# Splitting the mixed rows of routing weights into eight transfers and issuing the first weights from two queues

## The chip, the core and the metric

The kernel runs on one core of one Trainium2 chip. The metric is the device time of one execution in microseconds (us), and the time before is the median of three runs. Engines are called as the profile calls them: PE (TensorE matmul), PEld (its weight load), DVE (VectorE), ACT (ScalarE), POOL (GpSimd) and SP (SyncE, which issues the DMA transfers).

## What is computed

The reference takes x of 32 x 256 tokens of 128 numbers and adds two blocks to it, each behind a layer normalisation. Cut to what matters:

```python
# block 1: a selective state space layer, d_inner = 256, 16 states per channel
u, res = split(norm(x) @ W_in); u = silu(u)
delta = softplus(u @ W_delta + b_delta); Bm = u @ W_B; Cm = u @ W_C
h = exp(delta * A) * h + delta * Bm * u      # for every token in turn
y = (sum over states of h * Cm + u * D) * silu(res)
x = x + y @ W_out
# block 2: a mixture of 8 experts of 341 hidden units, 4 chosen per token, and one shared expert
weights = softmax of the 4 largest of norm(x) @ Wg + bias, 0 for the others
out = shared(norm(x)) + sum over experts of weights[e] * W3[e] (silu(W1[e] x) * (W2[e] x))
```

## The kernel before

The 8192 tokens are worked through in 16 tiles of 512. Every engine runs one long list of steps (`SP_ORDER`, `PE_ORDER`, `ACT_ORDER`, `DVE_ORDER`, `POOL_ORDER`); an entry such as `1:bbc.5` is step `bbc`, number 5, of tile 1. The lists interleave block 2 of one tile with block 1 of the next. Engines meet by semaphores alone, and an engine that waits holds up everything behind it in its list.

The nine experts (the shared one first) have 9 x 341 = 3069 hidden units, padded to 24 groups of 128 rows. They are laid in three groups of three experts; in each group six row groups belong to one expert whole, and the last two hold the 85 remaining units of each of the three experts, one after the other. A step `gated` on DVE multiplies two projections for a row group, `wmul` on POOL (L904) multiplies two row groups at once by the routing weight of their expert for each token, and `w3` on PE (L1331) projects them into `eo_bank`. Where both row groups are of one expert, SP spreads one row of 512 weights over 128 partitions (`wb`, L794, 256 KB). Where they are mixed (three steps per tile, 48 in all), `wb_mixed` of 2 x 128 partitions is filled from three rows, by four transfers whose partition counts stand in `SPANS` (L41): 85, 43, 42 and 85 (L804). There is one buffer `wb_mixed`, and the next fill waits until POOL has used it. The same `SPANS` cut the loads of W3 (L736).

Block 1 goes through `bbc` (L768): SP spreads two rows of Bm over 128 partitions (512 KB), POOL multiplies them into `hb` (`dbu`, L875), DVE runs the recurrence on `hb` (`scan`, L1077), and PE turns the result (`turn`, L1265). The buffers of `bbc` form a ring of four.

At the start SP issues x of tile 0, the small weights, then W1 and W2 (`load_w1_w2`, six transfers each, 1.5 MB each) and only then x of tile 1. DVE takes the statistics of tile 1 (`ln`, L1036), copies `c_sb` (L1070) and then splits W1 and W2 into a high and a low part (`split`, L1047 and L1049). POOL makes the scale of the normalisation of tile 1 from the statistics (`rstd`, L840 to L848) ahead of `delta` (L861), `du` (L866) and the first `dbu` of tile 0.

## Time and profile before

| | us |
|---|---|
| median of three runs | 1477.82 (1477.6 to 1478.57) |
| profiled execution | 1480.54 |
| its span on the core | 1478.7 |

| engine | busy in the span, us | share |
|---|---|---|
| PE | 1390.2 | 94% |
| DVE | 1297.3 | 88% |
| ACT | 1219.0 | 82% |
| POOL | 1193.2 | 81% |

The span is what the profile sees from the first instruction to the last; the profiled execution is 1.84 us longer. Busy shares are means over a start, a middle in which two tiles overlap, and an end; what the change may do is to be read from the places in which an engine stands idle and from what ended the wait. SP has no busy time of its own here: issuing a transfer or waiting isn't counted as work.

### The profile page before, as it was taken

The numbers are of one execution on the slowest core, as the hardware profiler recorded it, in microseconds if no ns is written. First come the engines' busy times: TensorE is split into PE (matmuls) and PEld (weight loads), VectorE is DVE, ScalarE is ACT, GpSimd is POOL, SyncE is SP. The second block draws the span as 40 slices with busy tenths as digits, with TensorE's granted clock in tenths as the row PEclk, the third lists the DMA queues.
The fourth block names the chain that finished last, engine by engine and source line by source line (L and its number), as shares of the span: only waits on it lengthen the run. The fifth ranks groups of instructions, "written<-read, shape, count | busy, mean of one in ns | idle before, by whom it ended". The sixth has DMA issues, their size and how long they took to land.

```text
span 1478.7 us, 28297 instructions
## 1 busy us (share of the span) xinstructions
PE 1390.2 (94%) x8950; PEld 1167.4 (79%) x8950; DVE 1297.3 (88%) x2444; ACT 1219.0 (82%) x1753; POOL 1193.2 (81%) x655
## 2 busy tenths in 40 slices
PE   5976699999999999999999999999899999999999
PEld 3854588888878888887878788787788878788888
DVE  3839899899989999999999999999899999989642
ACT  5977598888987989998888998999788889899431
POOL 5937697988969798988979889896898979697454
PEclk8987899999999999999999999999999999999999
DMA  6503141416144161514244051432314142232221
GB/s 176 159 8 107 66 127 58 145 45 170 46 123 129 43 174 44 172 37 143 88 111 126 32 186 51 138 100 86 121 59 146 37 151 94 83 119 77 67 67 49
DMA packets 88219, 146.40 MB, mean 99 GB/s; under 512 B 11306, under 2 KB 42791, under 8 KB 88071
## 3 DMA queue, kind: packets, MB, share of 16 engines
q1 hardware_dynamic: 88070, 144.59, 32.1%
q8 instruction: 73, 1.20, 0.3%
q14 instruction: 76, 0.61, 0.1%
HBM read 139.55 MB, written 5.01 MB: 98 GB/s over the span
## 4 chain that ended last, share of the span: by engine, by line
PE 59%; POOL 9%; DMA 9%; issue 9%; DVE 6%; ACT 5%; SPq 3%; DVEq 0%; POOLq 0%; ACTq 0%
PE eo_bank L1331 16%; PE turn L1265 9%; PE shared L1317 8%; PE shared L1319 8%; PE shared L1318 8%; POOL hb L875 4%; DMA bbc<-b_rows 4%; POOL gated L904 3%; DVE hb L1077 3%; PE shared L1222 3%; DMA wb_mixed<-w_rows 2%; DMA wb<-w_rows 2%; DVE acc L1089 2%; PE shared L1230 1%; PE shared L1293 1%
## 5 line engine op out<-in xcount | busy, mean ns | idle before, releaser
L1077 DVE TENSOR_TENSOR_SCAN hb<-decay,hb 128x512 f32<-128x512 f32 x512 | 607.4, 1213 | 43.8 <-POOL hb L875 36.2
L875 POOL TENSOR_TENSOR hb<-soft,bbc 128x1024 f32<-128x1024 f32 x256 | 605.9, 2383 | 48.0 <-issue 22.1
L1331 PEld LDWEIGHTS eo_bank<-w_sb,gated 128*128 128x128 f32 x3072 | 400.9, 193 | 65.1 <-POOL gated L904 24.7
L1331 PE MATMUL eo_bank<-w_sb,gated 128*128 128x128 f32 x3072 | 424.5, 277 | 18.8 <-POOL gated L904 18.6
L1011 ACT ACTIVATE decay<-delta,a_sb 128x510 f32<-128x510 f32 x512 | 342.6, 687 | 91.2 <-DVE hb L1077 88.5
L928 ACT ACT_TABLE_LOAD x315 | 404.1, 1283 | 5.6
L1089 DVE SCALAR_TENSOR_TENSOR acc<-turn,c_sb,acc 128x256 f32<-128x256 f32 x900 | 381.8, 476 | 16.0 <-PE turn L1265 15.2
L904 POOL TENSOR_TENSOR gated<-gated,wb 128x1024 f32<-128x1024 f32 x128 | 304.3, 2383 | 74.5 <-DVE gated L1159 48.9
L1265 PE MATMUL turn<-ident,hb 128*128 128x128 f32 x2048 | 304.9, 277 | 25.9 <-DVE acc L1089 16.4
L1265 PEld LDWEIGHTS turn<-ident,hb 128*128 128x128 f32 x2048 | 245.3, 143 | 79.1 <-issue 40.3
L1159 DVE TENSOR_TENSOR gated<-shared,s 128x512 f32<-128x512 f32 x384 | 257.3, 682 | 57.2 <-PE shared L1319 41.5
L1021 ACT ACTIVATE s<-shared 128x512 f32<-128x512 f32 x384 | 218.2, 597 | 103.8 <-PE shared L1319 80.3
L1317 PE MATMUL shared<-xh,w1h 128*128 128x512 f32 x384 | 176.2, 459 | 5.5 <-DVE gated L1159 5.0
L1317 PE MATMUL shared<-xh,w2h 128*128 128x512 f32 x384 | 177.3, 462 | 4.2 <-DVE gated L1159 3.6
L1319 PE MATMUL shared<-xh,w1l 128*128 128x512 f32 x384 | 152.9, 398 | 0.0
L1319 PE MATMUL shared<-xh,w2l 128*128 128x512 f32 x384 | 152.6, 397 | 0.0
L1318 PE MATMUL shared<-xl,w1h 128*128 128x512 f32 x384 | 152.4, 397 | 0.0
L1318 PE MATMUL shared<-xl,w2h 128*128 128x512 f32 x384 | 152.2, 396 | 0.0
L904 POOL TENSOR_TENSOR gated<-gated,wb_mixed 128x1024 f32<-128x1024 f32 x48 | 114.3, 2381 | 24.4 <-DMA wb_mixed<-w_rows 16.2
L1317 PEld LDWEIGHTS shared<-xh,w1h 128*128 128x128 f32 x384 | 73.4, 191 | 22.1 <-DVE gated L1159 8.6
L1319 PEld LDWEIGHTS shared<-xh,w1l 128*128 128x128 f32 x384 | 72.8, 190 | 17.6
L1319 PEld LDWEIGHTS shared<-xh,w2l 128*128 128x128 f32 x384 | 72.7, 189 | 17.5
(96 smaller groups left out, 1323.6 us busy)
## 6 DMA issues: line engine op xcount, KB each, us to landing
bbc<-b_rows SPq DMA_DIRECT2D x128, 512.0 KB, 5.8
wb<-w_rows SPq DMA_DIRECT2D x128, 256.0 KB, 6.6
wb_mixed<-w_rows SPq DMA_DIRECT2D x96, 170.0 KB
wb_mixed<-w_rows SPq DMA_DIRECT2D x48, 86.0 KB
x_in<-x_dram SPq DMA_DIRECT2D x16, 256.0 KB, 2.9
x_cur<-x_dram SPq DMA_DIRECT2D x16, 256.0 KB, 5.6
wb_mixed<-w_rows SPq DMA_DIRECT2D x48, 84.0 KB
out_dram<-o SPq DMA_DIRECT2D x15, 256.0 KB, 5.8
```

Of the source, the lines that this page charges most:

```text
L875: pool.tensor_tensor(hb[:, arg % HB_RING, :, :], du[:, h, :].unsqueeze(1).broadcast_to((P, GN, TOK)), bbc[:, r, :].rearrange("p (n t) -> p ...
L904: pool.tensor_tensor(tiles, tiles, weight, ALU.mult).then_inc(weighed, 1)
L928: act.preload_act_table_set(table)
L1011: act.activation(decay_bank[i][:, :].rearrange("p (b t) -> p b t", t=SEQ)[:, :, 1:], delta[:, h, :].rearrange("p (b t) -> p b t", t=SEQ)[: ...
L1077: dve.tensor_tensor_scan(states, decay_bank[i][:, :], states, 0.0, ALU.mult, ALU.add)\
L1089: dve.scalar_tensor_tensor(acc[:, blk, :], turn_bank[pair][:, i * DI:(i + 1) * DI], c_sb[:, blk, n:n + 1], acc[:, blk, :], ALU.mult, ALU.add)\
L1159: dve.tensor_tensor(gated[:, arg % GATED_RING, :], bank_of(t, "h2", arg)[:, :], s[:, arg % S_RING, :], ALU.mult).then_inc(gated_ready, 1)
L1265: mm = pe.transpose(turn_bank[pair][:, (NH * i + h) * P:(NH * i + h + 1) * P], src[:, blk * P:(blk + 1) * P], ident[:, :])
L1317: pe.matmul(dst[:, :], hi[:, cols], xh[:, :], start=True, stop=False)
L1318: pe.matmul(dst[:, :], hi[:, cols], xl[:, :], start=False, stop=False)
L1319: pe.matmul(dst[:, :], lo[:, cols], xh[:, :], start=False, stop=True).then_inc(full[step], 1)
L1331: mm = pe.matmul(eo_bank[:, blk * P:(blk + 1) * P], gated[:, k % GATED_RING, blk * P:(blk + 1) * P], w3_sb[:, k, :], start=(arg == 0 and k ...
```

## The change

`SPANS` gets eight entries instead of four: the pieces of 85, 43, 42 and 85 partitions become 80 + 5, 32 + 11, 32 + 10 and 80 + 5, with their place in the expert's remaining rows written out. Each piece has a semaphore of its own, so POOL waits for eight before a mixed `wmul`, and `w_out` on SP tests eight instead of four. The loads of W3 are cut the same way. The six transfers of W1 go from SP's list to ACT's, right behind its first table load; W2 stays on SP. Six waits on ACT name an earlier signal than before (the PE step that fills a bank in place of the engine that read it). The lists of steps are unchanged.

```diff
@@ -38,7 +38,8 @@
 WEIGHED = PAIRS - 1
 WHOLES = [q - 1 for q in range(1, PAIRS) if q % GROUP_PAIRS < GROUP]
 MIXED = [q - 1 for q in range(1, PAIRS) if q % GROUP_PAIRS == GROUP]
-SPANS = [(0, 0, REST, 0), (0, REST, P, 1), (1, 0, 2 * REST - P, 1), (1, 2 * REST - P, 3 * REST - P, 2)]
+SPANS = [(0, 0, 80, 0, 0), (0, 80, 85, 0, 80), (0, 85, 117, 1, 0), (0, 117, 128, 1, 32),
+         (1, 0, 32, 1, 43), (1, 32, 42, 1, 75), (1, 42, 122, 2, 0), (1, 122, 127, 2, 80)]
 
 HB_RING = 8
 BB_RING = 4
@@ -690,6 +691,18 @@
         SMALL = 8
         CONSTS = 8
         SUMS = 2 * FILLS - 4
+
+        def load_halves(eng, dst, src, landed, cleared):
+
+            eng.wait_ge(blank, cleared)
+            by_group = dst.rearrange("p (g c) -> p g c", g=GROUPS)
+            src_of = src.rearrange("p (g i c) -> p g i c", g=GROUPS, i=GROUP)
+            for grp in range(GROUPS):
+                eng.dma_start(by_group[:, grp, 0:GROUP * WHOLE].rearrange("p (i c) -> p i c", i=GROUP),
+                              src_of[:, grp, :, 0:WHOLE]).then_inc(landed, 16)
+                eng.dma_start(by_group[:, grp, GROUP * WHOLE:GROUP * HID].rearrange("p (i c) -> p i c", i=GROUP),
+                              src_of[:, grp, :, WHOLE:]).then_inc(landed, 16)
+
         block = ctx.enter_context(nc.Block())
 
 
@@ -709,18 +722,6 @@
                     sp_eng.dma_start(dst, src).then_inc(small_in, 16)
                 assert len(small) == SMALL
 
-            def load_w1_w2():
-
-                sp_eng.wait_ge(blank, 2)
-                for dst, src, landed in ((stage, w1_all, w1_in), (stage2, w2_all, w2_in)):
-                    by_group = dst.rearrange("p (g c) -> p g c", g=GROUPS)
-                    src_of = src.rearrange("p (g i c) -> p g i c", g=GROUPS, i=GROUP)
-                    for grp in range(GROUPS):
-                        sp_eng.dma_start(by_group[:, grp, 0:GROUP * WHOLE].rearrange("p (i c) -> p i c", i=GROUP),
-                                         src_of[:, grp, :, 0:WHOLE]).then_inc(landed, 16)
-                        sp_eng.dma_start(by_group[:, grp, GROUP * WHOLE:GROUP * HID].rearrange("p (i c) -> p i c", i=GROUP),
-                                         src_of[:, grp, :, WHOLE:]).then_inc(landed, 16)
-
             def load_w3():
 
                 sp_eng.wait_ge(blank, 3)
@@ -729,10 +730,8 @@
                     for j in range(WHOLE // P):
                         sp_eng.dma_start(w3_by_group[:, g_, j:2 * GROUP:2, :], w3_of[j * P:(j + 1) * P, g_, :, :])\
                             .then_inc(w3_in, 16)
-                taken = [0] * GROUP
-                for tile, lo, hi, i in SPANS:
-                    at = WHOLE + taken[i]
-                    taken[i] += hi - lo
+                for tile, lo, hi, i, at in SPANS:
+                    at += WHOLE
                     sp_eng.dma_start(w3_by_group[lo:hi, :, 2 * GROUP + tile, :], w3_of[at:at + hi - lo, :, i, :])\
                         .then_inc(w3_in, 16)
 
@@ -744,7 +743,7 @@
                         sp_eng.dma_start(x_in[:, :, :], x_t[:, TT * t:TT * (t + 1), :]).then_inc(x_in_sem, 16)
                         if t == 0:
                             load_small()
-                            load_w1_w2()
+                            load_halves(sp_eng, stage2, w2_all, w2_in, 2)
                     elif step == "load_cur":
                         wait_if(sp_eng, x1_ready, t)
                         carry_waits(sp_eng)
@@ -800,7 +799,7 @@
                                 sp_eng.wait_ge(consts, CONSTS)
                             wait_if(sp_eng, weighed, WEIGHED * (t + old // len(MIXED)) + MIXED[old % len(MIXED)] + 1)
                             carry_waits(sp_eng)
-                            for part, (tile, lo, hi, i) in enumerate(SPANS):
+                            for part, (tile, lo, hi, i, _) in enumerate(SPANS):
                                 sp_eng.dma_start(wb_mixed[lo:hi, tile, :],
                                                  rows[GROUP * grp + i, :].partition_broadcast(hi - lo))\
                                     .then_inc(wb_mixed_in[part], 16)
@@ -927,16 +926,16 @@
                         table = TABLE_OF[step]
                         act.preload_act_table_set(table)
                     if step == "xn":
-                        wait_if(act, xnT_ready, t)
+                        wait_if(act, full["xT"], t)
                         normalize("x", x_in, xn, t)
                     elif step == "x1n":
-                        wait_if(act, xl_ready, t)
+                        wait_if(act, full["x1T"], t)
                         normalize("x1", x1[:, t % 2, :, :], x1n, t)
                     elif step == "xT":
-                        wait_if(act, sres_ready, NH * t)
+                        wait_if(act, full["wi_res"], NH * t)
                         read_bank(t, step, arg, xnT[:, :], ACT.Copy, xnT_ready)
                     elif step == "x1T":
-                        wait_if(act, gate_steps, GATE_STEPS * t)
+                        wait_if(act, full["gate"], t)
                         read_bank(t, step, arg, x1nT[:, :], ACT.Copy, x1T_ready)
                     elif step == "xh":
 
@@ -948,8 +947,8 @@
                     elif step == "wi":
                         wait_if(act, du_ready, t)
                         wait_if(act, ud_ready, NH * t)
-                        wait_if(act, cbT_ready, t)
-                        wait_if(act, zb_ready, NH * t)
+                        wait_if(act, full["bt"], t)
+                        wait_if(act, full["dz"], NH * t)
                         read_bank(t, step, arg, u[:, arg, :], ACT.Silu, wi_ready)
                     elif step == "ud":
                         act.wait_ge(wi_ready, NH * t + arg + 1)
@@ -980,7 +979,7 @@
                         read_bank(t, step, arg, sres[:, arg, :], ACT.Silu, sres_ready)
                     elif step == "bt":
                         wait_if(act, b_stored, 16 * TT * t)
-                        wait_if(act, c_ready, t)
+                        wait_if(act, full["ct"], t)
                         act.wait_ge(full["bt"], t + 1)
                         act.activation(cbT[:, :], bank_of(t, "bt", 0)[:, 0:P], ACT.Copy).then_inc(cbT_ready, 1)
                     elif step == "wT":
@@ -1021,6 +1020,7 @@
                         act.activation(s[:, arg % S_RING, :], bank_of(t, "h1", arg)[:, :], ACT.Silu).then_inc(s_ready, 1)
 
             act.preload_act_table_set(EXP_TABLE)
+            load_halves(act, stage, w1_all, w1_in, 1)
             act.wait_ge(a_in, 16)
             act.activation(a_sb[:, :, :], a_sb[:, :, :], ACT.Exp).then_inc(a_exped, 1)
             act.wait_ge(consts, CONSTS)
```

SP's list in the middle of the program, at a mixed step of tile 1 (`wb` and `wb_mixed` carry routing weights, `bbc` carries Bm), before:

```order
L768 DMA bbc<-b_rows 128x1024 x2
L804 DMA wb_mixed<-w_rows 85x512
L804 DMA wb_mixed<-w_rows 43x512
L804 DMA wb_mixed<-w_rows 42x512
L804 DMA wb_mixed<-w_rows 85x512
L794 DMA wb<-w_rows 128x512 x2
L768 DMA bbc<-b_rows 128x1024
```

and now:

```order
L767 DMA bbc<-b_rows 128x1024 x2
L803 DMA wb_mixed<-w_rows 80x512
L803 DMA wb_mixed<-w_rows 5x512
L803 DMA wb_mixed<-w_rows 32x512
L803 DMA wb_mixed<-w_rows 11x512
L803 DMA wb_mixed<-w_rows 32x512
L803 DMA wb_mixed<-w_rows 10x512
L803 DMA wb_mixed<-w_rows 80x512
L803 DMA wb_mixed<-w_rows 5x512
L793 DMA wb<-w_rows 128x512 x2
L767 DMA bbc<-b_rows 128x1024
```

Eight issues stand where four stood, ahead of the same transfers. The start of ACT's list now (`gated` is the memory in which W1 waits to be split):

```order
L1022 ACT_TABLE_LOAD
L701 DMA gated<-w_all_dram 128x3x256
L703 DMA gated<-w_all_dram 128x3x85
L701 DMA gated<-w_all_dram 128x3x256
L703 DMA gated<-w_all_dram 128x3x85
L701 DMA gated<-w_all_dram 128x3x256
L703 DMA gated<-w_all_dram 128x3x85
L1025 ACTIVATE a_sb<-a_sb 128x32
```

Before, these six stood on SP between the small weights and W2, and ACT had nothing between its table load and `a_sb`.

## Rows read from the trace of the kernel before

**Rows 1.** Busy time by stretch, the middle: us, then each engine, PEclk, DMA share, GB/s.
```profile
240.00:1365.00 1125.00, 1097.12 (x7113) 920.31 (x7111) 1068.41 (x2029) 995.17 (x1392) 964.86 (x515) 1.00 0.33 102
```

**Rows 2.** Waits of POOL: who, for what, us in total, times, longest.
```profile
POOL gated L904 <- DMA wb<-w_rows: 24.6, 8, 6.1
POOL hb L875 <- issue: 22.1, 6, 5.2
...
POOL gated L904 <- DMA wb_mixed<-w_rows: 16.2, 7, 5.0
```

**Rows 3.** Line L804: issue ns min/median/max; then L768, bbc: issue to landing.
```profile
L804 SPq DMA_DIRECT2D wb_mixed<-w_rows x192: 258/297/1426, 134.9 to 1454.9; - x192
...
DMA to landing us min/median/max: 3.3/5.8/14.2
```

**Rows 4.** Chain of waits at 1362 us: start, us, what.
```profile
1362.02 10.52 DMA wb_mixed<-w_rows
```

**Rows 5.** Busy time by stretch around that transfer, columns as in group 1.
```profile
1361.00:1364.00 3.00, 3.00 (x19) 2.47 (x18) 3.00 (x5) 2.87 (x5) 0.98 (x1) 1.00 0.93 281
...
1370.00:1373.00 3.00, 2.99 (x21) 2.52 (x19) 3.00 (x6) 1.40 (x3) 0.30 (x1) 1.00 0.08 30
```

**Rows 6.** Timeline of POOL at two waits: start, us, what, [idle before, what ended it].
```profile
149.50 2.34 POOL L875 TENSOR_TENSOR hb<-soft,bbc 128x1024 f32<-128x1024 f32 x1 [4.71 <-issue]
...
269.05 2.35 POOL L904 TENSOR_TENSOR gated<-gated,wb_mixed 128x1024 f32<-128x1024 f32 x1 [2.57 <-DMA wb_mixed<-w_rows]
```

**Rows 7.** Timeline of PE at the six places of the middle and the end.
```profile
271.45 1.16 PE L1331 MATMUL eo_bank<-w_sb,gated 128*128 128x128 f32 x8 [2.35 <-POOL gated L904]
...
444.64 0.50 PE L1317 MATMUL shared<-xh,w2h 128*128 128x512 f32 x1 [3.01 <-DVE gated L1159]
...
782.83 0.71 PE L1331 MATMUL eo_bank<-w_sb,gated 128*128 128x128 f32 x4 [1.58 <-POOL gated L904]
...
1242.34 0.63 PE L1265 MATMUL turn<-ident,hb 128*128 128x128 f32 x4 [1.39 <-DVE acc L1089]
...
1299.79 1.16 PE L1331 MATMUL eo_bank<-w_sb,gated 128*128 128x128 f32 x8 [1.71 <-POOL gated L904]
...
1375.10 2.04 PE L1331 MATMUL eo_bank<-w_sb,gated 128*128 128x128 f32 x8 [2.11 <-POOL gated L904]
```

**Rows 8.** Busy time by stretch behind two of these places.
```profile
270.00:276.00 6.00, 4.55 (x17) 3.73 (x18) 2.75 (x5) 3.18 (x4) 6.00 (x3) 0.72 0.30 104
...
1375.00:1378.00 3.00, 2.90 (x11) 2.71 (x12) 0.00 (x0) 0.00 (x0) 3.00 (x3) 0.53 0.40 66
```

**Rows 9.** Chain of waits at the start: x of tile 1, from its issue to its landing.
```profile
13.71 5.89 DMA x_in<-x_dram
```

**Rows 10.** Busy time by stretch at the start, columns as in group 1.
```profile
6.00:9.00 3.00, 2.66 (x22) 2.47 (x21) 0.00 (x0) 1.65 (x4) 0.64 (x2) 1.00 0.64 132
...
12.00:15.00 3.00, 3.00 (x8) 1.33 (x7) 0.00 (x0) 2.31 (x4) 0.00 (x0) 1.00 1.14 315
```

**Rows 11.** Timeline of the start: PE, then DVE, then POOL.
```profile
18.74 0.30 PE L1247 MATMUL shared<-ident,cbT 128*128 128x128 f32 x1 [0.49 <-ACT cbT L985]
...
20.70 0.19 DVE L1070 COPY c_sb<-shared 128x64 f32<-128x64 f32 x1
...
22.59 3.36 DVE L1049 TENSOR_TENSOR w1l<-gated,w1h 128x3072 fp32r<-128x3072 f32 x1
...
27.65 3.36 DVE L1049 TENSOR_TENSOR w2l<-hb,w2h 128x3072 fp32r<-128x3072 f32 x1
38.31 2.34 DVE L1077 TENSOR_TENSOR_SCAN hb<-decay,hb 128x512 f32<-128x512 f32 x2 [7.30 <-POOL hb L875]
...
22.68 3.32 POOL L842 TENSOR_SCALAR negm_x<-mv_x 128x4 f32<-128x4 f32 x1
...
31.03 2.34 POOL L861 TENSOR_TENSOR delta<-delta,soft 128x1024 f32<-128x1024 f32 x1
```

**Rows 12.** DMA issues by line: KB each, median us from issue to landing.
```profile
b_rows<-cbT SPq DMA_DIRECT2D x64, 8.0 KB, 1.4
```

## The prediction

> **What bounds the kernel now.** I read the busy time by stretch first. In the middle, from 240 to 1365 us, PE is busy for 1097 of 1125 us and DVE for 1068 [rows 1]: two engines near their limit, with 28 us of idle time on PE. A gain there must come from places where both stand still, so the next view is who makes them wait. POOL is the engine between them, and its waits [rows 2] name transfers three times: 24.6 us for `wb`, 16.2 us for `wb_mixed`, and 22.1 us before `hb` that the profile calls "issue". These last I count as waits for `bbc`: a `dbu` needs only `bbc`, `du` and free `hb` buffers, and nothing on an engine ended then.
>
> The transfers explain the length of these waits. The chain at 1362 us runs through the last of four `wb_mixed` transfers, which takes 10.52 us from issue to landing [rows 4]. Its three mates were issued right before it, and all four bring 255 rows of 2 KB, 510 KB. A `bbc` of 512 KB lands in 3.3 us when nothing lies ahead of it, and in up to 14.2 us [rows 3]. Size is not the reason. The reader is to compare the DMA share in the first and the last 3 us of the transfer: 0.93 of the 16 DMA engines at first, 0.08 at the end [rows 5]. 0.08 of 16 is little more than one engine: the fill ends with one DMA engine working through its part while the others have nothing left. Rows of 85 and 43 partitions are evidently not dealt out evenly to 16 engines, and whatever is issued behind them lands late too.
>
> **Mixed rows, the main term.** 80 and 32 partitions divide by 16, and the pieces left over are 5, 11, 10 and 5. If the 510 KB are dealt out evenly, the fill lands no sooner than a lone `bbc` (3.3 us) and no later than now (10.5 us). Four more issues at the median of 0.30 us [rows 3] come on top, 1.2 us. I take a landing about 5 us earlier: 7.2 us of possible gain less 1.2, less 1 because the DMA engines are nearly full of other traffic at the beginning [rows 5]. Transfers queued right behind gain some 4 us.
>
> What that is worth I read where POOL stood waiting with a mixed fill in flight, and what PE lost behind it:
> - At 149.5 us POOL waits 4.71 us for the `bbc` issued right behind the first mixed fill, then runs one more `wmul` for which PE waits [rows 6]: 4.7 us.
> - At 269 us POOL waits 2.57 us for the fill itself [rows 6], and PE idles 2.35 us. At five more places PE idles 3.01, 1.58, 1.39, 1.71 and 2.11 us behind the same pattern [rows 7]; sometimes DVE stands between POOL and PE, as at 444.6 and 1242.3 us. The six gaps are 12.15 us.
> - Behind the first and the last of them PE's granted clock is lower, 0.72 over 6 us and 0.53 over 3 us [rows 8], which is the lower of its two levels (1.2 and 2.4 GHz) for part of the time; PE had stood idle just before in both. (1 - 0.72) x 6 + (1 - 0.53) x 3 = 3.1 us, if PE had worked through all of it.
>
> That is 4.7 + 12.15 + 3.1 = 20.0 us if every one of these vanishes and nothing takes its place. The other end is zero. I take two thirds, 13.3 us: DVE and PE idle together at most of these places, so the loss is real, but PE has only 28 us of idle time in the whole middle and DVE 57 [rows 1], and the lists keep an order in which the next wait is often for another engine. Work that piled up in a pause will in part wait elsewhere.
>
> The price is on SP. 48 mixed fills with four more issues make 48 x 1.2 = 58 us of SP's time, hidden behind the waits in which SP stands anyway; where it isn't hidden, the next `bbc` or `wb` is issued 1.2 us later and still lands earlier than now. Four more tests ahead of `w_rows` in each tile, and four more semaphores ahead of 48 `wmul` (the queue of POOL tests them while the multiplication before still runs), I put at 1 us in all, between 0 and 3.
>
> **W1 on ACT's queue, and the start.** x of tile 1 is issued at 13.71 us, behind W1 and W2, and lands 5.89 us later, at 19.6 us [rows 9]. From 12 to 15 us the DMA engines are full at 315 GB/s, from 6 to 9 us they move 132 GB/s [rows 10]. With W1 issued from ACT right behind its first table load, the empty part is filled: at least 3 us x (315 - 132) GB/s = 0.55 MB, which is 1.7 us less to do later, and about twice that if the 3 us before are as empty. I take 3 us: x of tile 1 lands at about 16.6 us. For the six issues on ACT I put nothing: its own first work waits for x and the scale of tile 0, and idles longer than six issues take. The small weights share the DMA engines with W1 now; tile 0 needs them only some us later.
>
> What follows is less than 3 us. DVE then waits for `ct` from PE, which ends at 18.74 + 0.30 = 19.04 us, instead of x, and copies `c_sb` at 19.2 instead of 20.70 us [rows 11]: the split is 1.5 us earlier. POOL makes the scale of tile 1 before the split begins and not beside it. Beside it, an operation on four numbers per partition took 3.32 us, from 22.68 to 26.00 us, and ended with DVE's subtraction, which took 3.36 us from 22.59 us [rows 11]. So POOL stands still while DVE splits. The page "SBUF — State Buffer" of the Trainium skill (section "SBUF: two separate sides") states it as a lock on a shared port, held for a whole instruction, against a DVE instruction with two inputs in SBUF; by that rule `delta` and `du` can't run beside the split either, and the start gains about 1.5 us and no more. The trace agrees as far as the small operations show it.
>
> `delta` starts at 31.03 us, when the split ends at 27.65 + 3.36 = 31.01 us, and the first recurrence at 38.31 us after an idle time of 7.30 us on DVE [rows 11]. The low end is thus 1.5 us (POOL still waits for the split's end); the high end 1.5 + 7.3 = 8.8 us (`delta`, `du` and `dbu` fit beside the split). I take 2.5 us, near the low end, since the row shows POOL stopped; the extra 1 us is for ACT, which no longer has tile 1's normalisation between the split and its first decays. The moved waits on ACT cost and save nothing: none of the signals that they replace ended a wait of ACT that counts.
>
> **The sum.** 13.3 + 2.5 - 1 = 14.8 us off the profiled execution of 1480.5 us, 1465.7 us. The median of the runs lies 2.7 us below that execution, so the prediction is **1463 us**.
>
> **Rivals.**
> - *Mostly hidden.* Only the waits that the profile ascribes to `wb_mixed` vanish. On PE these are the gaps at 271, 783 and 1375 us, 2.35 + 1.58 + 2.11 = 6.0 us [rows 7]; two thirds are 4 us: 1474 us. For it speaks that 16.2 of POOL's waits bear that name and 24.6 us the name of `wb` [rows 2], many of these right behind `w_rows` with no fill ahead. Against it, that the `bbc` behind a fill lands late as well [rows 3, 6]. Chance 0.16, of which 0.06 ends within 3 us of no change; that the pieces aren't dealt out evenly after all, so that nothing happens, is in it with 0.02.
> - *More than that.* All 20 us come off, and POOL works beside the split: 20 + 8.8 = 28.8 us off 1477.8 us, 1449 us. Against it stands the row of POOL stopped beside the split, and that lists kept as they are rarely give back every gap. Chance 0.12.
> - *Slower: eight issues delay what stands behind them.* POOL's 8 + 6 + 7 waits for transfers [rows 2] each become 1.2 us longer, 25 us on POOL; a third of it reaching PE is 8 us: 1486 us. It decides if the landing of a fill gains less than the 1.2 us that its issue loses. The page "DMA: Bandwidth & Descriptors" of the Trainium skill (section "Rules for kernel authors") says to join many small transfers into a large one, since under 64 KB one pays mostly overhead; six of the eight pieces are 64 KB or less, so by this rule the case would be likely. Against it stands that transfers of 8 KB land in 1.4 us [rows 12], less than half the time of a `bbc` alone, and are issued one right behind the other: their overheads overlap. Chance 0.06.
>
> The forecast keeps 0.66.
>
> **The numbers.** A measurement of this kernel tells about 0.2% (3 us) from no change. Faster by more: 0.66 + 0.12 + 0.10 = 0.88; within: 0.06; slower: 0.06. The range runs from 1451 us, most of the way to the larger case, to 1474 us, where only the named waits go; outside lie most of the slower case, the smallest effects and the far end of the larger one, together less than 0.2.
>
> **What would show it.** Right: POOL's waits for `wb_mixed` near zero and those for `wb` and "issue" at most half; the longest landing of a `bbc` well under 14.2 us; PE's gaps at the six places gone or under 1 us, its clock whole there; x of tile 1 landed near 16.6 us, POOL's scale of tile 1 done before the split, the first recurrence at about 36 us. Wrong: POOL's waits for transfers vanish and the span hardly moves (then POOL wasn't what held PE, and waits for DVE or for PE's own list will have grown by the same amount); or the fills still take 10 us; or the longest waits now stand behind SP's eight issues.

## The result, and the profile after

The changed kernel takes **1445.99 us** (median of four runs, 1444.51 to 1446.87) against 1478.19 us for the kernel before, run beside it (1477.6 to 1483.46): a ratio of 0.9773, 95% interval [0.975, 0.9797]. I had forecast 1463 us with a range of 1451 to 1474. The sign is right and the size is not: 32 us came off where I expected 15, and the time lies below the range. The profiled execution took 1446.87 us, its span 1445.1 us, 33.6 us less than before.

The page's first part, then the shares of the chain that ended last (by engine):

```profile
PE 1381.1 (96%) x8950; PEld 1164.5 (81%) x8950; DVE 1296.5 (90%) x2444; ACT 1218.0 (84%) x1753; POOL 1194.7 (83%) x655
...
PE 74%; DVE 9%; issue 6%; ACT 4%; POOL 3%; DMA 2%; SPq 1%; DVEq 0%; ACTq 0%; POOLq 0%
```

PE's busy time fell by only 9 us (1390.2 before), its idle time by some 25 us (1478.7 - 1390.2 = 88.5 before, 64.0 now). On the chain, PE's share rose from 59% to 74%, while DMA fell from 9% to 2% and POOL from 9% to 3%. The middle of the span, to compare with [rows 1] (us, then busy us of PE, PEld, DVE, ACT and POOL, then PEclk, DMA share, GB/s):

```profile
240.00:1330.00 1090.00, 1077.86 (x7042) 908.19 (x7042) 1056.26 (x2008) 983.89 (x1379) 958.14 (x509) 1.00 0.33 104
```

PE stands idle for 12 of 1090 us here, against 28 of 1125. Who waits on POOL, to compare with [rows 2] (us in total, times, longest):

```profile
POOL gated L903 <- DMA wb<-w_rows: 24.4, 8, 5.5
...
POOL hb L874 <- DMA bbc<-b_rows: 14.4, 5, 7.0
...
POOL hb L874 <- PE turn L1265: 6.9, 3, 3.8
POOL hb L874 <- issue: 5.5, 3, 2.8
```

No wait for `wb_mixed` is left (16.2 us before), and "issue" fell from 22.1 to 5.5 us. The waits for `wb` are as long as before, 24.4 us, while I had named a fall to half as a sign of being right: they don't follow the fills. Now the transfers: the eight pieces (line L803, issue ns and landing us, min/median/max), then `bbc` (L767), to compare with [rows 3]:

```profile
L803 SPq DMA_DIRECT2D wb_mixed<-w_rows x384: 269/321/1124, 133.6 to 1422.9; - x192
...
DMA to landing us min/median/max: 1.8/2.8/6.6
...
DMA to landing us min/median/max: 3.3/4.8/8.6
```

A piece lands within 6.6 us, where the one of [rows 4] took 10.52, and the longest `bbc` takes 8.6 instead of 14.2 us. The DMA engines during the first mixed fill of tile 14, the last but one (issued from 1331.40, landed at 1337.62; columns as above), show why. It is the same fill as in [rows 5]:

```profile
1331.00:1334.00 3.00, 3.00 (x19) 2.51 (x18) 3.00 (x5) 2.73 (x4) 0.63 (x1) 1.00 0.85 269
1334.00:1337.00 3.00, 3.00 (x21) 2.43 (x20) 3.00 (x6) 2.97 (x5) 3.00 (x2) 1.00 0.77 245
1337.00:1340.00 3.00, 3.00 (x23) 2.74 (x23) 3.00 (x6) 2.97 (x4) 1.22 (x2) 1.00 0.55 184
```

The share is 0.85 and 0.77 while the fill is in flight, where it had run down from 0.93 to 0.08; the third row already holds what comes behind it. The long tail at a share of little more than one engine is gone.

Next the places of [rows 6] and [rows 7]. Of the six gaps of PE, five are gone altogether and one has 0.36 us left (430.80, the one of 3.01 us at 444.64). At the two places of POOL no idle time is recorded any more. This is POOL's timeline, then the PE gap that is left behind the first place (2.26 us, where it was 6.99 at 154.20 us before, so the 4.7 us forecast there came off):

```profile
143.38 2.36 POOL L874 TENSOR_TENSOR hb<-soft,bbc 128x1024 f32<-128x1024 f32 x1
...
260.32 2.40 POOL L903 TENSOR_TENSOR gated<-gated,wb_mixed 128x1024 f32<-128x1024 f32 x1
...
148.10 0.99 PE L1331 MATMUL eo_bank<-w_sb,gated 128*128 128x128 f32 x4 [2.26 <-POOL gated L903]
```

PE's granted clock, which had been at its lower level for 3.4 us from 166.9, 3.4 us behind the gap at 271 us, 6.8 us from 1040.7 and 3.4 us from 1375, is at the lower level for one stretch of 3.4 us at 1022 in the whole of 166 to 1445 us.

The start went otherwise than forecast (the chain's row of x of tile 1; busy time from 6 to 9 us; then DVE and POOL, to compare with [rows 9 to 11]):

```profile
11.99 6.59 DMA x_in<-x_dram
```

```profile
6.00:9.00 3.00, 3.00 (x18) 3.00 (x17) 0.18 (x1) 1.77 (x5) 0.74 (x2) 1.00 1.18 311
```

```profile
19.68 0.19 DVE L1070 COPY c_sb<-shared 128x64 f32<-128x64 f32 x1
...
26.64 3.36 DVE L1049 TENSOR_TENSOR w2l<-hb,w2h 128x3072 fp32r<-128x3072 f32 x1
37.30 2.34 DVE L1077 TENSOR_TENSOR_SCAN hb<-decay,hb 128x512 f32<-128x512 f32 x2 [7.31 <-POOL hb L874]
...
19.95 1.64 POOL L839 TENSOR_SCALAR veps_x<-mv_x 128x4 f32<-128x4 f32 x1 [13.13 <-DVE mv_x L1040]
21.67 3.32 POOL L841 TENSOR_SCALAR negm_x<-mv_x 128x4 f32<-128x4 f32 x1
...
30.01 2.34 POOL L860 TENSOR_TENSOR delta<-delta,soft 128x1024 f32<-128x1024 f32 x1
```

The DMA engines are full from 6 us on (311 GB/s, before 132), as meant. But x landed at 18.6, not 16.6 us, and the first recurrence starts at 37.30 instead of 38.31 us: 1.0 us gained, not 2.5. POOL still makes its scale beside the splits (`negm_x` again takes 3.32 us). A cost that I had put at nothing shows here, too: `a_sb`, which now shares the DMA engines with W1, lands at 7.03 instead of 4.56 us, and ACT starts tile 0's normalisation behind it at 7.19 instead of 6.84 us (6.88 in e1 below, where W1 stays on SP).

I matched every instruction of PE in the two traces and read how far it moved (the lists have the same length and order). The table sums that by stretch of the span before, in us, for the changed kernel and for six of the runs below, which the next section explains.

```
stretch before    changed   e2     e3     e6     e5     e4     e9
   0 to   45       -1.2    -0.9   -1.5   -1.3   -1.6   -0.9   -0.2
  45 to  130       -0.1     0.0   +1.8   -0.2   +0.1   -0.8   +1.5
 130 to  200       -4.8     0.0   -1.0   -1.7   -3.5   -4.8   -4.5
 200 to  300       -4.1    -2.0   -1.8   -2.7   -4.1   -4.0   +1.3
 300 to  600       -4.4    -2.0   -4.1   -5.4   -5.2   -4.3   +1.5
 600 to  800       -2.7    +1.8   -1.1   -2.9   -3.1   -3.1   +3.8
 800 to 1070       -5.2    -0.1   -2.1   -6.0   -7.4   -1.9   -4.8
1070 to 1475      -11.2    -0.2   -2.2   -9.6  -10.6   -6.6   +1.1
sum               -33.7    -3.3  -12.0  -29.7  -35.3  -26.4   -0.2
```

One row of the changed kernel stood nowhere in my prediction: 5.2 us between 800 and 1070, nearly all of it between 1034 and 1066. Single entries of a microsecond or two are to be read with care: e2 has the old pieces and the old time, and still moves by up to 2.0 us in a stretch.

### The profile page after: what moved, and what is told of

Its sections match the earlier page's. It is cut to its first block, busy times and chain, and to the rows that moved or that the text cites. A ratio compares the mean times of both kernels' runs of the same rounds, so it can differ in the third digit from the quotient of the medians.

```text
span 1445.1 us, 28645 instructions
## 1 busy us (share of the span) xinstructions
PE 1381.1 (96%) x8950; PEld 1164.5 (81%) x8950; DVE 1296.5 (90%) x2444; ACT 1218.0 (84%) x1753; POOL 1194.7 (83%) x655
## 4 chain that ended last, share of the span: by engine, by line
PE 74%; DVE 9%; issue 6%; ACT 4%; POOL 3%; DMA 2%; SPq 1%; DVEq 0%; ACTq 0%; POOLq 0%
PE eo_bank L1331 20%; PE turn L1265 12%; PE shared L1317 10%; PE shared L1319 10%; PE shared L1318 10%; DVE hb L1077 5%; PE shared L1222 3%; DVE acc L1089 2%; PE shared L1230 2%; PE shared L1293 2%; POOL hb L874 1%; ACT L927 1%; POOL gated L903 1%; PE eo_bank L1276 1%; PE shared L1276 1%
## 5 line engine op out<-in xcount | busy, mean ns | idle before, releaser
L874 POOL TENSOR_TENSOR hb<-soft,bbc 128x1024 f32<-128x1024 f32 x256 | 606.9, 2389 | 27.9 <-DMA bbc<-b_rows 14.4
L903 POOL TENSOR_TENSOR gated<-gated,wb_mixed 128x1024 f32<-128x1024 f32 x48 | 114.7, 2389 | 10.3 <-DVE gated L1159 10.2
L1319 PEld LDWEIGHTS shared<-xh,w2l 128*128 128x128 f32 x384 | 72.2, 188 | 17.3
```

The lines of the kernel that those rows point to most:

```text
L874: pool.tensor_tensor(hb[:, arg % HB_RING, :, :], du[:, h, :].unsqueeze(1).broadcast_to((P, GN, TOK)), bbc[:, r, :].rearrange("p (n t) -> p ...
L903: pool.tensor_tensor(tiles, tiles, weight, ALU.mult).then_inc(weighed, 1)
L1319: pe.matmul(dst[:, :], lo[:, cols], xh[:, :], start=False, stop=True).then_inc(full[step], 1)
```

## The experiments

Each run was timed beside the kernel before, whose median was 1479.87 us for e1 to e4, 1480.59 for e5 to e8, 1480.22 for e9 to e11 and 1480.92 for e12, against 1478.19 above. So between these groups, and against the changed kernel, the ratios compare better than the times.

**One part alone.** e1 is the kernel before with the eight even pieces and nothing else. e2 is the changed kernel with the four old pieces:

```diff
 # e2, against the changed kernel
-SPANS = [(0, 0, 80, 0, 0), (0, 80, 85, 0, 80), (0, 85, 117, 1, 0), (0, 117, 128, 1, 32),
-         (1, 0, 32, 1, 43), (1, 32, 42, 1, 75), (1, 42, 122, 2, 0), (1, 122, 127, 2, 80)]
+SPANS = [(0, 0, 85, 0, 0), (0, 85, 128, 1, 0), (1, 0, 42, 1, 43), (1, 42, 127, 2, 0)]
```

> The kernel before with nothing changed but the eight even pieces (routing weights and W3); W1 stays on SP, ACT's waits as before. Theory (the even pieces free the last DMA engine, W1 on ACT gives only the 1.2 us that the start moved): 1447 us, ratio 0.979. Rival (W1 from ACT, or the earlier signals that ACT waits for, bring the part of the gain that the prediction missed, about 15 us): 1462 us, ratio 0.99.

> The changed kernel with the four old pieces of 85, 43, 42 and 85 put back; W1 on ACT and ACT's new waits stay. Theory: 1.0 to 1.3 us below before, about 1477 us, ratio 0.999, with POOL's waits as before. Rival (as in the first run): about 1463 us.

e1 took 1447.02 us, ratio 0.9778 [0.9764, 0.9791]; e2 1478.65 us, ratio 0.9991 [0.9981, 1.0001] (its profiled execution lies 3 us lower than the one before, its median doesn't). The pieces are the change; W1 on the second queue and ACT's new waits are worth about 1 us, and by the interval 3 at most. In e1 DVE's first recurrence starts at 38.33 us as before, in e2 at 37.38 us as in the changed kernel, so the 1.0 us of the start is W1's.

**Even, or just more?** The length of a fill, here and below, is the time from the first issue to the last landing of its pieces, the median over the 48 fills. Rows per DMA engine follow from how many engines each transfer shows at its landing: 85 rows go to 5 engines, 43 to one, 42 to 14, 80 and 32 to 16. Which engines these are the traces don't name, but one, called engine 0 here, must be in all: in each of the 48 fills before, the pieces land one after the other, the 43 rows 3.9 us behind the first 85, the 42 (3 on an engine) 0.24 us behind these and the last 85 (17 on an engine) another 1.4 us later (medians), some 0.08 to 0.09 us per row. This engine gets 17 + 43 + 3 + 17 = 80 of 255 rows before, 18 in the changed kernel. (The others are counted as if a transfer always took the first ones.) The page "DMA: Bandwidth & Descriptors" of the Trainium skill (section "Why a DMA increments its semaphore by 16 and not by 1") gives the rule: the largest number up to 16 that divides the slowest dimension (of more than one element) on both sides. The trace agrees in each of these sizes. e3 has eight pieces, too, cut so that engine 0 still gets 80 rows (75 + 10 + 37 + 6 + 29 + 13 + 75 + 10). e4 leaves the second and third fill of each tile in four old pieces and cuts only the first evenly.

> The changed kernel with eight pieces per mixed fill that are cut badly on purpose: 75, 10, 37, 6, 29, 13, 75, 10 partitions. 37 and 29 have no divisor up to 16, so if a transfer uses the largest number of engines up to 16 that divides its partitions, one engine gets 5 + 1 + 37 + 1 + 29 + 1 + 5 + 1 = 80 of the 255 rows, as many as with the four old pieces (17 + 43 + 3 + 17), and 18 with the changed kernel's pieces. Theory (what counts is the fullest engine): 1476 to 1481 us, like before less the start, fills that end 10 to 12 us after their issue. Rival (smaller or more pieces bring the gain): 1446 us.

> The changed kernel in which only the first of a tile's three mixed fills is cut into eight even pieces; the second and the third use the four old pieces. Theory (the gain comes from a few places, nearly all behind a tile's first fill, whose use follows its issue by 11 to 17 us, where the second and third have 15 to 25 us): 5 to 7 us slower than the changed kernel, 1451 to 1453 us; what comes back is mainly at tile 12's second fill (1.6 us) and behind tile 10's second (2.4 us). Rival (a shorter time in the queue helps everywhere alike): a third of the gain, 1467 us.

e4 came close to what was expected, 0.7 us above the range: 1453.72 us, 0.9823 [0.981, 0.9836]. The first fill of a tile carries most of the gain; in most tiles of the kernel before it is issued 11 to 17 us ahead of its multiplication, the second and third mostly 14 to 25 us. e3 fell between theory and rival: 1468.35 us, 0.9921 [0.9908, 0.9935]. Its fills last 10.0 us (10.6 before), and `bbc` lands within 11.9 us of its issue (14.2 before). So number alone does little to a fill, and yet a third of the gain came with fills that are 0.6 us shorter: PE's gaps of over 0.3 us behind 165 us sum to 24.7 us against 30.8, and the time at the lower clock behind 200 us fell from 13.6 to 6.8 us. Besides the 80 rows on engine 0, e3 takes load off engines 1 to 4 (37 rows before, at most 14 in e3). Whether that, the order of the pieces or the 1.5 us more that SP takes to issue them brought this third stays open, so the fullest engine is shown for the length of a fill and not for all of the time.

**How even is enough?** e5 and e6 have six pieces each, with 40 rows on each of five engines, and 58 rows on one.

```diff
 # pieces of a fill, rows
-80 + 5 + 32 + 11 + 32 + 10 + 80 + 5
+85 + 32 + 11 + 32 + 10 + 85            # e5: engines 0 to 4 get 40
+80 + 5 + 43 + 42 + 80 + 5              # e6: engine 0 gets 58
```

> The mixed fill in six pieces, 85 + 32 + 11 + 32 + 10 + 85 rows: the two pieces of 85 still go to five engines (17 rows each), the middle is even, so engines 0 to 4 get 40 rows each of a fill and the rest get 4 to 6. Theory (the time follows the rows on the fullest engine: 80 gave 1468 to 1479, 18 gave 1447): a fill lasts about 7 us and the time is about 1454 (1450 to 1459), better than 58 rows on one engine. Rival (what matters is that some engines carry the load at all, or that the load is taken off engines 1 to 4): 1462 or more, no better than the kernel with 58 rows on engine 0 alone.

> The mixed fill in six pieces, 80 + 5 + 43 + 42 + 80 + 5 rows: the big pieces are even, the middle one of 43 rows goes to engine 0 alone, so engine 0 gets 58 rows and no other more than 14. Theory (rows on the fullest engine): a fill lasts about 8.5 us, the time is about 1461 (1456 to 1466), some 7 us over the kernel with 40 rows on five engines. Rival (the five-engine pieces were the harm, the single-engine piece is not): 1450 or less, under the kernel with 40.

e5 took 1445.72 us, 0.9761 [0.9745, 0.9777], the whole gain; e6 1450.74 us, 0.9796 [0.9779, 0.9813]. The order of the two is the theory's; both are far faster than I expected, as I had drawn a straight line through the times. Fills get shorter with every step, the times do not. (A fill is counted as landing at its use if its last piece lands within 0.5 us ahead of POOL's multiplication.)

```
rows on the fullest engine       80   80 (e3)   58 (e6)   40 (e5)  18 (changed)
median fill, us                10.6      10.0       7.8       6.4           5.2
first fill of a tile, us       11.8      11.6      10.1       7.9           6.1
fills landing at their use        8         8         5         2             0
PE gaps over 0.3 us            30.8      24.7       9.4       6.2           8.3
time, us                     1478.2    1468.4    1450.7    1445.7        1446.0
ratio to before              1.0000    0.9921    0.9796    0.9761        0.9773
```

A row on the fullest engine lengthens a fill by (10.0 - 7.8) / 22 = 0.10 us from 58 to 80 rows, and by 0.08 and 0.05 us in the steps below. From 10.6 to 7.8 us of fill, each us is worth 10 us of time; below 6.4 us nothing is left to gain. That is the shape of a due time: the fill, with what is issued behind it, has to be there when POOL comes. The traces bear it out: POOL stands idle for 16.5 us at the eight fills that land at their use before, and for 0.02 us at the two that still do in e5.

**Is a transfer behind the fill what is late?** e9 is the kernel before, uneven pieces and all, with `bbc` issued ahead of a fill at the 18 places where it had come within 3 us behind one. One of them:

```diff
-10:wbc.0.1 12:b_out.0 10:wbc.2.3 12:bbc.0 10:wbc.4 12:bbc.1
+10:wbc.0.1 12:b_out.0 12:bbc.0.1 10:wbc.2.3.4
```

> The kernel before with its four uneven pieces, and one thing moved: at the 18 places where an input broadcast bbc is issued on SP within 3 us behind a mixed fill, it is issued ahead of the fill. The fills stay as long (10.6 us); what stood behind them no longer does. Theory (part of the 33 us came from bbc transfers that had waited behind a fill's long pieces on the same DMA engines, which my prediction didn't count, above all near 1034 to 1066): 8 to 15 us faster than before, 1465 to 1472, with the 5 us near 1034 to 1066 gone and POOL's waits for wb_mixed still near 16 us. Rival (the fills' own lateness is all that counts): no change, 1477 to 1481, or slower, as the fills then start later.

The time stayed, 1480.24 us, ratio 1.0001 [0.9988, 1.0014], so my 8 to 15 us fell. The table of stretches shows two effects that cancel. From 130 to 200 us e9 gains 4.5, and from 800 to 1070 us 4.8, as much as the changed kernel does there. From 200 to 800 and behind 1070 us it loses 7.7 us, where the fills are issued later and POOL waits longer for them. (Ahead of 130 us nothing was moved; the 1.5 us there are the spread between traces.) POOL's waits in e9:

```profile
POOL gated L903 <- DMA wb_mixed<-w_rows: 29.7, 10, 5.9
...
POOL hb L874 <- issue: 9.2, 3, 4.9
```

"issue" fell from 22.1 to 9.2 us, and `wb_mixed` rose from 16.2 to 29.7. So both readings hold, each at its own places: at those two it is the `bbc` behind the fill that is late, elsewhere the fill itself. Moving all 18 doesn't serve both, and a shorter fill does; moving `bbc` at those two places alone wasn't tried. e9 also tells what the profile's name hid. This is POOL before, near 1034 and 1055 us:

```profile
1034.30 4.68 POOL L875 TENSOR_TENSOR hb<-soft,bbc 128x1024 f32<-128x1024 f32 x2 [4.04 <-PE turn L1265]
...
1055.06 2.40 POOL L875 TENSOR_TENSOR hb<-soft,bbc 128x1024 f32<-128x1024 f32 x1 [4.43 <-issue]
```

and the PE gap that follows the first of them, and the stretch behind it, in which PE runs at 1.2 GHz (PEclk 0.50):

```profile
1039.76 0.50 PE L1317 MATMUL shared<-xh,w1h 128*128 128x512 f32 x1 [3.64 <-DVE gated L1159]
```

```profile
1040.70:1047.50 6.80, 6.16 (x23) 5.45 (x23) 5.22 (x9) 3.76 (x5) 6.80 (x4) 0.50 0.51 145
```

The `bbc` needed at 1034.30 was issued at 1023.64, 0.9 us behind a fill, and its last part landed at 1034.18, after 10.5 us. In the changed kernel the same one takes 5.9 us. The profile put the wait down to a PE step, I passed over it, and PE's 3.64 us and half of 6.8 us at the lower clock went uncounted. (In the changed kernel 0.83 us of this gap and 3.4 us at the lower clock are left.)

**The price of an issue.** e10 has the fill in twelve even pieces, 18 rows on the fullest engine as in eight, and four more issues (48 + 32 + 5, 16 + 16 + 11, 16 + 16 + 10, 48 + 32 + 5).

> The changed kernel with the mixed rows in twelve even pieces (48+32+5, 16+16+11, 16+16+10, 48+32+5 rows): the rows per engine stay as in eight, the issues of SP grow by four per fill, some 1.5 us. Six pieces with at most 40 rows on one engine already gave the whole gain. Theory (SP's issues and the number of transfers are hidden): 1445 to 1448. Rival (the count of transfers is a price of its own, which fewer rows per engine only outweighs): 1451 or more.

The result is the rival's: 1452.74 us, 0.981 [0.9785, 0.9835], 7 us over eight pieces by the medians and 5.5 by the ratios. (The two intervals overlap by 0.001; the slowest run of the changed kernel and of e1 took 1448.94 us, the fastest of e10 1451.46.) A fill takes 4.8 us to issue (3.0 in eight pieces, 1.3 in four), and SP reaches the next transfer later. The fills themselves last 6.3 us, as long as in e5, where that cost nothing. At the same place the `dbu` behind a first fill waits longer (POOL in the changed kernel, then in e10):

```profile
426.44 2.40 POOL L874 TENSOR_TENSOR hb<-soft,bbc 128x1024 f32<-128x1024 f32 x1 [2.51 <-issue]
```

```profile
429.75 2.39 POOL L873 TENSOR_TENSOR hb<-soft,bbc 128x1024 f32<-128x1024 f32 x1 [3.98 <-issue]
```

In both the `bbc` lands just before (426.32 and 429.63 us). PE loses 1.4 us behind this place, of the 8.8 us between the two traces; the largest part, 3.1 us, lies between 650 and 700 us. This is the mechanism of my slower rival, with too little weight to show at eight. The Trainium skill's page "DMA: Bandwidth & Descriptors" (section "Rules for kernel authors") advises joining small transfers; the runs agree from eight to twelve and disagree from four to eight, where evenness was worth some 30 us more than the issues cost.

**The start.** e7 issues x of tile 1 ahead of W2. e8 does that as well and moves the split of W1 on DVE from before the first recurrence to behind tile 0's last; the waits that count the splits change with it.

```diff
 # e7, SP, tile 0 and tile 1
                             load_small()
+                        elif t == 1:
                             load_halves(sp_eng, stage2, w2_all, w2_in, 2)
 # e8 besides, DVE
-0:c.0 0:split.0.1 0:scan0.0
+0:c.0 0:split.1 0:scan0.0
...
-3:ln.0 0:x1.0
+3:ln.0 0:split.0 0:x1.0
```

> The changed kernel with tile 1's x issued ahead of W2. Its x should land near 13 instead of 18.6, so that the small operations of its normalization are done before DVE's splits begin. If x's landing is what the first recurrence hangs on (my prediction's reasoning), the first recurrence starts some 5 us sooner, near 32 in the span, and the time falls by 3 to 5 us to about 1442. Rival: the splits themselves keep POOL's operations from running beside them, whenever x lands; the first recurrence then stays at 36 to 37.5 and the time at 1445 to 1446.5.

> As the kernel with tile 1's x first, but one of the two 6.7 us splits moves on DVE from before the first recurrence to before tile 0's gate input (W2's is then the first, W1's the later). If DVE's splits are what delays the first recurrence, it starts near 31 instead of 37.3 and the time falls by 4 to 6 us against the changed kernel, to about 1441. Rival: the split costs DVE the same 6.7 us wherever it stands, since DVE and TensorE's queue behind it are both full from there on: less than 2 us of gain, 1444.5 or more.

e7: 1447.41 us, 0.9774 [0.9757, 0.9791], no gain. Its x landed at 13.89 us and POOL's scale was done at 17 us, yet the first recurrence starts at 36.22 us. DVE and POOL of e7 show why:

```profile
21.33 3.36 DVE L1050 TENSOR_TENSOR w1l<-gated,w1h 128x3072 fp32r<-128x3072 f32 x1
24.60 3.91 DVE L1048 CAST w2h<-hb 128x3072 fp32r<-128x3072 f32 x1
28.54 5.38 DVE L1050 TENSOR_TENSOR w2l<-hb,w2h 128x3072 fp32r<-128x3072 f32 x1
36.22 5.83 DVE L1078 TENSOR_TENSOR_SCAN hb<-decay,hb 128x512 f32<-128x512 f32 x5 [2.30 <-POOL hb L875]
```

```profile
22.61 4.28 POOL L861 TENSOR_TENSOR delta<-delta,soft 128x1024 f32<-128x1024 f32 x1 [5.62 <-ACT soft L1003]
26.97 3.74 POOL L866 TENSOR_TENSOR soft<-delta,u 128x1024 f32<-128x1024 f32 x1
```

Each takes as long as the rest of the other engine's instruction plus its own: `delta` 24.69 - 22.61 + 2.34 = 4.4 us (4.28 recorded), the cast 26.89 - 24.60 + 1.75 = 4.0 (3.91), `du` 28.51 - 26.97 + 2.35 = 3.9 (3.74), the subtraction 30.71 - 28.54 + 3.36 = 5.5 (5.38). They take turns, instruction by instruction. The page "SBUF — State Buffer" of the Trainium skill (section "SBUF: two separate sides") calls it an exclusive lock that whoever starts first holds for the whole instruction; the trace agrees, and in both directions: here DVE waits for POOL as well. So what POOL does beside the splits, DVE pays back.

e8 came out between: 1443.31 us, 0.9744 [0.9728, 0.976], 2.7 us less than the changed kernel and 4.1 less than e7, which was run beside it. Its first recurrence starts at 32.40 us, 4.9 us sooner than in the changed kernel: about one split, which takes 1.75 + 3.36 = 5.1 us and not the 6.7 that I had expected. 3 to 4 us of that are still there at the end.

**A version that beats the changed kernel.** In e8 POOL idles 8.0 us for `bbc.5` of tile 1, which stands on SP behind `w_out` of tile 0 and its wait for ACT. e11 moves `bbc.5` and `bbc.6` ahead of `w_out`; e12 is e11 with the six pieces of e5.

```diff
-1:bbc.3.4 2:b_out.0 0:w_out.0 0:wbc.0 1:bbc.5 0:wbc.1.2 1:bbc.6 0:wbc.3.4.5
+1:bbc.3.4 2:b_out.0 1:bbc.5.6 0:w_out.0 0:wbc.0.1.2.3.4.5
```

> The kernel with tile 1's x first and one split moved behind tile 0's recurrences (1443.3), and on SP tile 1's bbc.5 and bbc.6 moved ahead of tile 0's w_out, behind whose wait of 13 us for the routing weights they stood. In that kernel POOL idles 8.0 us near 135 for bbc.5, and TensorE 3.5 and 1.8 us. Theory: POOL's wait goes, and 4 to 8 us of TensorE's idle time between 129 and 158 with it, 1436 to 1440. Rival: TensorE waits there for the routing weights anyway, the order of its work is fixed, and the idle time moves to the next place: 1442 to 1444.

> The last version (tile 1's x first, one split later, tile 1's bbc.5 and bbc.6 ahead of w_out, 1441.3) with the six pieces of 85 + 32 + 11 + 32 + 10 + 85 rows instead of eight. With the changed kernel's order six and eight gave the same time. Theory (40 rows on the fullest engine are as good as 18, two issues less are worth under 1 us): 1440 to 1442. Rival (twelve issues cost 7 us, so issues near eight already cost 1 to 2 us each pair, hidden in the comparison before by the longer fills): under 1439.

e11 took 1441.3 us, 0.9738 [0.9716, 0.976]; e12 1439.82 us, **0.9721 [0.9708, 0.9734]**. POOL in e8 and in e11, then PE in e11:

```profile
135.14 4.66 POOL L875 TENSOR_TENSOR hb<-soft,bbc 128x1024 f32<-128x1024 f32 x2 [8.00 <-DMA bbc<-b_rows]
```

```profile
117.30 11.69 POOL L875 TENSOR_TENSOR hb<-soft,bbc 128x1024 f32<-128x1024 f32 x5
...
148.30 4.64 POOL L875 TENSOR_TENSOR hb<-soft,bbc 128x1024 f32<-128x1024 f32 x2 [7.84 <-PE turn L1266]
```

```profile
147.04 1.94 PE L1266 MATMUL turn<-ident,hb 128*128 128x128 f32 x8 [3.45 <-DVE acc L1090]
```

POOL's wait for `bbc` went, and POOL now stands 7.84 us for PE 13 us further on. PE gained 5.3 us on e8 up to 150 us, and lost 4.4 of them again by 165 us, where it now waits for DVE. This is the case of "hidden" for one wait: the expected 4 to 8 us were not there, and e11 by itself can't be told from e8. e12 came out 0.2 us below the expected range, not under the 1439 us of its rival, and can't be told from e11; it is 6 us under the changed kernel's time, 0.5% by the ratios. In its middle PE is busy for 1159.6 of 1170 us, so what is left lies mainly in the first 160 us, with 46 of 59 us of its idle time:

```profile
160.00:1330.00 1170.00, 1159.59 (x7560) 977.40 (x7560) 1133.73 (x2158) 1057.23 (x1481) 1030.04 (x548) 1.00 0.33 103
```

## Why the prediction was wrong in size

The mechanism held in the main: one DMA engine's share of 80 rows set when a fill, and what stood behind it, landed, and at the named places that held up POOL, then DVE, then PE. (The third of the gain that came in e3, with 80 rows still on one engine, isn't explained by it.) The price was wrong, term by term, against 14.8 us forecast and 33.7 us measured from profile to profile. What the traces give is good to half a microsecond or so, as it hangs on where a stretch is cut:

- **"I take two thirds"** failed: +6.7 us. The reason given was that work piled up in a pause would wait elsewhere. It didn't: at the six places PE's gaps are gone, and of POOL's waits for transfers only those named `bbc` grew, from 7.4 to 14.4 us, while "issue", `wb_mixed` and `hb` behind PE fell by 43 us together (16.6, 16.2 and 10.3). Nothing was given back between the places either: from 800 to 1034 us PE's lead stays at 17.1 to 17.3 us. DVE and PE had stood idle together, and both made up for it.
- **The full sum of 20.0 us** was itself too small at the places I had named, where the matched instructions show 23.0 us: +3.0 us. Most of it lies at the last three (9.6 us against 6.6 by gaps and clock): around a gap that I read stand smaller ones.
- **The place from 1034 to 1066 us** was left out: +5.2 us. [rows 3] said that a `bbc` could take 14.2 us to land, but I counted such waits by the name that the profile gave them, and here it named a PE step. e9 shows that this place hangs on the transfer behind the fill.
- **Waits under a microsecond**, 0.3 to 1.5 us at a time between 300 and 1220 us, weren't counted: 4.3 us together. They are a lesson about sums over listed gaps: what is under the list's last row adds up.
- **The start**, 2.5 us forecast, 1.2 measured: -1.3 us. x landed at 18.6 us. I had the DMA engines' empty part right (132 to 311 GB/s) and the order wrong: x still stood behind W2 on SP, where the last issues took 0.85 to 1.87 us each. The small weights, which I took to be needed only some us later, now share the DMA engines with W1: `a_sb` landed 2.5 us later, tile 0 started 0.35 us later, and `ct` ends at 19.45 instead of 19.04 us. e7 shows that an earlier x would hardly have helped: the splits and POOL take turns.
- **Costs of 1 us** on SP and POOL don't show in the sum: +1.0 us. e10 shows that more issues do cost time, and that twelve pieces are too many.

14.8 + 6.7 + 3.0 + 5.2 + 4.3 - 1.3 + 1.0 = 33.7 us. As to the landing, "about 5 us earlier" was right (10.6 to 5.2 us).

Of the rivals, the larger case came nearest by its number (1449 us) but not by its reason: all that it added to the middle was less than what was there, and its 8.8 us at the start didn't come. The case that only the waits named `wb_mixed` vanish fell; so did the slower one at eight pieces, and at twelve its mechanism is there. My range ended 5 us above the time because its low end leaned on that larger case: all 20 us of the gaps that I had listed and most of 8.8 us at the start, with no room for gaps that I had not listed.

## What to carry to other kernels

When the DMA share runs down to one engine at the end of a transfer, count the rows that each engine gets, over all transfers that are waited for together, and cut the partition counts until the fullest engine is near the mean. Here 40 rows of 255 on one engine were as good as 18, so stop cutting where the time stops falling: each further piece costs SP 0.3 to 0.4 us, and twelve pieces gave back 5 to 7 us. To price such a change, follow every transfer that is issued behind the slow one, whatever name the profile gives to the wait, and match the instructions of the two traces afterwards to see where the time came off. If the two engines near the limit stand idle at the same moment, count the whole pause.

## What was unexpected of the hardware

- The time falls steeply and then stops: from fills of 10.6 to 7.8 us the kernel gained 28 us, from 6.4 to 5.2 us nothing.
- A `bbc` of 512 KB behind a fill can hang on one part: of the one issued at 1023.64 us the first of 16 parts landed at 1027.14, the fifteenth at 1031.10 and the last at 1034.18 us, 10.5 us after its issue. The quickest `bbc` took 3.3 us.
- The pieces of a fill queue one behind the other on one engine: before, they land in the order of issue in all 48 fills, 3.9, 0.24 and 1.4 us apart for 43, 3 and 17 rows of 2 KB.
- At the splits DVE and POOL take turns by whole instructions, in both directions. A cast of 1.75 us took 3.91 us beside `delta`.
- In the changed kernel, issuing the last transfers of W2 and x of tile 1 took SP 0.85 to 1.87 us each, from 8.9 to 14 us in the span, with the DMA engines full. The first two of W2, at 7.3 us and with the engines full as well, took 0.43 and 0.49 us; what made the difference isn't shown.
